# Normalisations and the last feed-forward group of a two-layer network stack, moved from between the stages into the steps around them

## The chip, the cores and the metric

The kernel runs on one core of one Trainium2 chip. The metric is the device time of one launch in microseconds. The time before is 2357.35 us, the median of 3 runs (2354.39 to 2360.7).

The core's engines run their own instruction queues in order and meet through semaphores: TensorE (PE; matrix products and transposes into the eight PSUM banks), VectorE (DVE), ScalarE (ACT), GpSimd (POOL) and SyncE (SP), which issues the DMAs here. A wait in a queue holds all that stands behind it in that queue.

## The reference

`x` is 16 batches of 128 tokens by 128 features, and so is `ctx`. All is float32.

```python
x = x + L0_xattn(layernorm(x), ctx, ctx)   # 16 heads of 8 features
x = x + L0_ffn(layernorm(x))               # "first network", depth 6
x = x + L1_xattn(layernorm(x), ctx)        # two attentions and a gate
x = x + L1_ffn(layernorm(x))               # "second network", depth 2

# one layer of a network (window 32 and 16 heads, or window 64 and 8 heads):
q, k, v = split(shift_tokens(x) @ Wqkv)    # l2-normalised q, k; rotary
x = local_attention(q, k, v) @ Wo + x
h = layernorm(shift_tokens(x)) * g + b
a, gate = split(h @ W1 + b1)               # 341 columns each
x = (a * gelu(gate)) @ W2 + b2 + x

# second cross-attention:
c2s = softmax(Qc Ks^T) Vs;  s2c = softmax(Qs Kc^T) Vc
g = sigmoid([c2s, s2c] Wg + bg);  result = g * c2s + (1 - g) * s2c
```

The layernorms in the second, third and fourth of these lines are the three "normalisations between stages" below; they have no learnt factors. Batches don't depend on each other, but a feed-forward works on a group of four batches (512 columns), and each cross-attention of the second kind on a pair (256 columns).

## The kernel before

The activations lie features by tokens in SBUF, `base_x` (the residual of a stage) and `z` (the input of a stage and the running value inside a network), each 128 partitions by 2048 columns: 16 batches, 4 groups, 8 pairs. `arena` is one large tile cut into 49 slots of 512 columns; each stage names its buffers as slots of it.

**First cross-attention.** A software pipeline over 16 batches, `for s in range(NB + 2)` on each engine (TensorE from L577 on): step s does the scores of batch s, turns probabilities of s-1 and s-2, and does the values and the output projection of s-2. `X0["res"]` counts the batches whose residual is in `base_x`.

**A normalisation between stages** (`ln_pe`, `ln_dve`, `ln_act`, L240 to L312) is done for all four groups at once: TensorE multiplies each group by a matrix of 1/128 (L231), VectorE subtracts the mean (L272), ScalarE squares (L263), TensorE gets the variances (L237), VectorE does a reciprocal square root as 11 small operations, each waiting on the last (L281 to L296, `RSQ`), TensorE spreads it over the partitions with 16 transposes (L245), and VectorE multiplies into `z` (L303). It starts when the last batch or pair of the stage before is done (`X0["res"]` is 16, `FF["outer"]` is 4, `YP["gt"]` is 32), and its banks are 0 to 7, so nothing else of TensorE goes on beside it.

**First network** (`PHASES[0]`): steps s = 0 to 103. Step s projects batch s mod 16 of layer s div 16 (L659), with rotary, norm and transposes of s-1, scores and values of s-2 and the output projection of s-3. A feed-forward group takes four steps in bank 2, from step 7 on (`ff_phase`): mean, variance and root in the first (and the down product of the group before), broadcast and first gate product in the second, two gates in the third with the gelus, three up products in the fourth. Group 23, the last, has its steps at 99 to 103, where no attention work is left. The l2 norm's Newton steps use bank 2 too (`nt`, `normal_free`). Then VectorE adds `z` to `base_x` (L1685), four times, and the normalisation follows. The transposes of the second cross-attention's weights stand there as well (L1064).

**Second cross-attention**: 11 steps over 8 pairs. Step s: projections of pair s (L1074, L1082), scores, row maximum, exponentials, row sums of s-1, values of s-1 (L1091) and outputs of s-2 (L1120), gate of s-3 (L1128; VectorE L2015 to L2023).

**Second network** (`PHASES[1]`): steps 96 to 117 with two batches a step and the feed-forward in bank 2 from step 101 on.

**SyncE** loads each batch shifted by a token from `z` into `hs` by DMA (L481, L482). Before each network it waits until all four groups of `z` are normalised (`LN["xn"]` 8 and 16).

The order of all work is written out by hand: it is the order of the calls in each engine's loops.

## Time and profile before

| | us |
|---|---|
| median of 3 runs | 2357.35 |
| profiled execution | 2356.19 |
| its span | 2354.4 |
| TensorE busy | 2149.5 |
| VectorE busy | 1740.5 |
| ScalarE busy | 1708.9 |
| GpSimd busy | 1338.4 |

The span is the time between the first and the last instruction of the profiled execution; the device time of the same execution is 1.8 us more. "Busy" is the time in which an engine had an instruction under way; it says nothing of where in the span. Views used are the page, the chain of waits (followed back from the last instruction to what released each), windows (busy time and TensorE's granted clock, as a share of 2.4 GHz, in a stretch), groups of instructions, and the timeline.

### The profile page before, as it was taken

Reading aid. Unit: us, or ns where it says so; the run is one execution under the profiler, and the core shown is the slowest. Engines: PE = TensorE matmul, PEld = TensorE weight load, DVE = VectorE, ACT = ScalarE, POOL = GpSimd, SP = SyncE. Lnnn points to the kernel's source line nnn. Section 1 sums busy time; section 2 is a strip of 40 time slices with the busy share of each in tenths; the row PEclk is TensorE's granted clock in tenths of the full one; section 3 lists DMA queues with packets and bytes.
Section 4 is the critical chain, followed back from the end, with each engine's and each line's share of the span. In section 5 each row is a group of like instructions: output and inputs, shape, how many; then the busy total and the mean of one; then the engine's idle time right before and its main releaser. Section 6 shows DMA issues by size and latency. Waiting matters only on the chain.

```text
span 2354.4 us, 88151 instructions
## 1 busy us (share of the span) xinstructions
PE 2149.5 (91%) x33770; PEld 1463.6 (62%) x33770; DVE 1740.5 (74%) x4827; ACT 1708.9 (73%) x5908; POOL 1338.4 (57%) x1270
## 2 busy tenths in 40 slices
PE   6988999999999999999999999999998696899997
PEld 4664766666666666666666666666666383566663
DVE  3868878778777777877787777778774276788873
ACT  3756878887777787778787878778876252788783
POOL 1317766666666666666676666666673033766660
PEclk8988999999999999999999999999999797999999
DMA  4001221112211221112211122112111100000000
GB/s 109 3 4 29 71 58 47 40 48 65 56 43 42 60 55 49 43 43 69 57 47 40 46 64 56 43 42 56 48 43 38 37 1 10 13 13 15 15 10 23
DMA packets 141518, 96.92 MB, mean 41 GB/s; under 512 B 61832, under 2 KB 133040, under 8 KB 141104
## 3 DMA queue, kind: packets, MB, share of 16 engines
q1 hardware_dynamic: 141104, 91.28, 15.3%
q8 instruction: 274, 4.49, 0.8%
q14 instruction: 140, 1.15, 0.2%
HBM read 23.11 MB, written 1.05 MB: 10 GB/s over the span
## 4 chain that ended last, share of the span: by engine, by line
PE 78%; issue 7%; ACT 7%; DVE 6%; POOL 2%; SPq 0%; DMA 0%; ACTq 0%; POOLq 0%; DVEq 0%
PE bank L659 22%; PE bank L770 8%; PE bank L680 7%; PE bank L737 6%; PE bank L714 5%; PE bank L828 4%; PE bank L807 4%; PE bank L723 3%; PE bank L817 3%; PE bank L708 2%; PE bank L589 2%; ACT arena L1296 1%; PE bank L597 1%; PE bank L610 1%; ACT L1296 1%
## 5 line engine op out<-in xcount | busy, mean ns | idle before, releaser
L659 PE MATMUL bank<-wqkv,hs 128*128 128x512 f32 x1344 | 673.2, 619 | 33.1 <-ACT arena L1271 15.2
L1512 POOL TENSOR_TENSOR arena<-arena,rnorm 128x512 f32<-128x512 f32 x448 | 454.3, 1042 | 382.0 <-DVE rnorm L1754 380.8
L1505 POOL TENSOR_TENSOR arena<-arena 128x512 f32<-128x512 f32 x448 | 567.0, 1273 | 168.0 <-DVE arena L1705 167.7
L1240 ACT ACTIVATE arena<-bank,amx 128x64 f32<-128x64 f32 x1536 | 457.6, 334 | 7.1 <-DVE amx L1769 6.7
L1700 DVE TENSOR_TENSOR arena<-bank,rot 128x512 f32<-128x512 f32 x448 | 307.0, 685 | 87.1 <-PE bank L659 83.1
L659 PEld LDWEIGHTS bank<-wqkv,hs 128*128 128x128 f32 x1344 | 230.2, 192 | 221.8 <-issue 160.3
L1217 ACT ACTIVATE arena<-bank 128x512 f32<-128x512 f32 x448 | 263.9, 616 | 124.1 <-PE bank L680 123.0
L1240 ACT ACTIVATION_READ_ACCUMULATOR arena<-bank,amx 128x1 f32 x1536 | 351.0, 229 | 0.0
L1705 DVE TENSOR_TENSOR arena<-bank,rot 128x256 f32<-128x256 f32 x896 | 333.8, 414 | 0.0
L1211 ACT ACTIVATE arena<-bank 128x512 f32<-128x512 f32 x448 | 264.9, 645 | 69.0 <-DVE arena L1705 68.3
L680 PEld LDWEIGHTS bank<-ident,arena 128*128 128x128 f32 x1792 | 213.3, 142 | 156.2 <-issue 125.4
L1712 DVE TENSOR_REDUCE ss<-arena 128x8 f32<-128x512 f32 x448 | 283.7, 670 | 32.5 <-ACT arena L1211 32.1
L1519 POOL TENSOR_TENSOR arena<-arena,ainv 128x512 f32<-128x512 f32 x192 | 200.2, 1043 | 160.5 <-DVE ainv L1777 160.5
L680 PE MATMUL bank<-ident,arena 128*128 128x128 f32 x1792 | 252.0, 275 | 18.3 <-POOL arena L1512 11.8
L770 PEld LDWEIGHTS bank<-arena,wo 128*128 128x128 f32 x1792 | 221.8, 195 | 55.9 <-issue 48.8
L1271 ACT ACTIVATE arena<-bank 128x256 f32<-128x256 f32 x384 | 127.2, 387 | 169.0 <-PE bank L737 168.7
L770 PE MATMUL bank<-arena,wo 128*128 128x128 f32 x1792 | 226.9, 279 | 3.3 <-ACT arena L1271 2.6
L737 PE MATMUL bank<-arena 64*64 64x32 f32 (+1 forms) x9216 | 185.4, 221 | 42.2 <-issue 41.3
L737 PEld LDWEIGHTS bank<-arena 64*64 64x64 f32 x9216 | 160.7, 135 | 67.3 <-issue 50.3
L1769 DVE TENSOR_REDUCE amx<-bank 128x4 f32<-128x256 f32 x384 | 143.9, 416 | 43.9 <-PE bank L714 43.6
L714 PE MATMUL bank<-arena 64*32 64x64 f32 (+1 forms) x12288 | 168.7, 217 | 0.0
L714 PEld LDWEIGHTS bank<-arena 64*32 64x32 f32 x12288 | 154.8, 105 | 0.2
(171 smaller groups left out, 3208.3 us busy)
## 6 DMA issues: line engine op xcount, KB each, us to landing
arena<-arena SPq DMA_DIRECT2D x768, 64.0 KB
wqkv<-in_L_ffn_Wqkv_dram SPq DMA_DIRECT2D x24, 256.0 KB, 3.2
hs<-z SPq DMA_DIRECT2D x128, 32.0 KB, 1.8
fx<-z SPq DMA_DIRECT2D x32, 128.0 KB, 2.2
hs<-z SPq DMA_DIRECT2D x128, 31.8 KB, 1.9
fx<-z SPq DMA_DIRECT2D x32, 127.0 KB, 2.5
wqkv<-in_L_ffn_Wqkv_dram SPq DMA_DIRECT2D x24, 128.0 KB, 2.6
w<-in_L_ffn_W_dram SPq DMA_DIRECT2D x6, 341.0 KB
```

What stands on the lines that cost most here:

```text
L659: nc.tensor.matmul(bank[o][:], src[:], wqkv[w][:, off:off + 512], start=True, stop=True).then_inc(AT[name] if part < 2 else AT[name][i], 1)
L680: mm = nc.tensor.transpose(bank4[o][:, j, :], rc[i][c][p % 2][:, j * P:(j + 1) * P], ident[:])
L714: mm = nc.tensor.matmul(bank[3 + g][q:q + 32, DH * j:DH * j + n], q_t[i][rows, P * j + q:P * j + q + 32], k_t[i][rows, P * j + key:P * j + ...
L737: mm = nc.tensor.matmul(bank4[7 - half][to:to + DH, j, q0:q1], src[g][rows, DH * h:DH * h + DH], pbt[i][0][rows, h * P + q0:h * P + q1], s ...
L770: mm = nc.tensor.matmul(bank4[7][:, 0, :], wo[w][:, i, j, :] if ni == 0 else wo[w][:, j // 2, j % 2, :], o_t[i][:, j * P:(j + 1) * P], sta ...
L1211: nc.scalar.activation(sq[i][c], bank[c][:], ACT.Square).then_inc(AT["sqk" if c else "sqq"], 1)
L1240: ins = nc.scalar.activation(pb[i][0][p % 2][:, h * DH:(h + 1) * DH], bank[3 + g][:, j * DH:(j + 1) * DH], ACT.Exp, bias=amx[p % 2][:, i, ...
L1505: nc.gpsimd.tensor_tensor(t, t, rs[i][c], ALU.add).then_inc(AT["ak" if c else "aq"][i], 1)
L1512: nc.gpsimd.tensor_tensor(t, t, rnorm[p % 2][:, i, HU * c:HU * c + HU].unsqueeze(2).to_broadcast([P, HU, DH]), ALU.mult).then_inc(AT["mk" ...
L1700: nc.vector.tensor_tensor(heads(rc[i][c][p % 2]), src, r[:, 2 * c, :].unsqueeze(1).to_broadcast([P, HU, DH]), ALU.mult)
L1705: ins = nc.vector.tensor_tensor(dst, src[:, :, (1 - a) * hd:(2 - a) * hd], r[:, 2 * c + 1, a * hd:(a + 1) * hd].unsqueeze(1).to_broadcast( ...
L1712: nc.vector.tensor_reduce(ss[:, i, HU * c:HU * c + HU], heads(sq[i][c]), AX.X, ALU.add).then_inc(AT["ssk" if c else "ssq"], 1)
```

## The change

Each normalisation between stages is done group by group, and its instructions are placed inside the steps of the stage before or after. The number of products, transposes and elementwise operations on full blocks is the same; the chain of 11 small VectorE operations is done once a group (4 columns wide instead of 16), so 12 times for three normalisations instead of 3. Which group goes where:

| for | groups 0 to 3 |
|---|---|
| first network | 0 in steps 6, 7, 8 of the first cross-attention; 1, 2, 3 in steps 1-2, 3-4, 5-6 of the network |
| second cross-attention | 0 and 1 in steps 96 and 97 of the first network; 2 and 3 in steps 2-3 and 5-6 of the cross-attention |
| second network | 0 and 1 in steps 7 and 9 of the cross-attention; 2 and 3 in steps 97 and 99 of the network |

Step 17 of the first cross-attention stands inside step 0 of the first network. The first network's steps end at 98; what steps 99 to 103 held (feed-forward group 23) stands in steps 1 to 5 of the second cross-attention, which gets a step without a new pair (`y_pair`) and so has 12. Its steps 10 and 11 stand behind step 96 of the second network. Buffers of the two cross-attentions get other slots of `arena`, and its values go to bank 7 instead of 2. SyncE waits for the group it needs.

```diff
-        x_q, x_k, x_v = (big[:, i * TOK:(i + 1) * TOK] for i in range(3))
+        x_q, x_k, x_v = (arena[:, (4 + i) * TOK:(5 + i) * TOK] for i in range(3))
...
+        def y_pair(t):
+            return t if 0 <= t < 6 else t - 1 if 7 <= t < 9 else -1
...
+        def g_mean(pe, n, k, o):
+            nc.tensor.matmul(bank[o][:], mean_w[:], group(base_x, k), start=True, stop=True).then_inc(LN["mean"], 1)
+        def g_var(pe, n, k, o):
+            pe.wait_ge(LN["sq"], NBLK + n + 1)
+            for j in range(4):
+                mm = nc.tensor.matmul(bank[o][:, 2 * j:2 * j + 2], g_sq[n % 2][:, j * P:(j + 1) * P], mean_w[:, 0:2],
+                                      start=True, stop=True)
+            mm.then_inc(LN["var"], 1)
+        def g_broadcast(pe, n, k, o):
+            pe.wait_ge(ln_rsqrt, (n + 2) * RSQ)
+            pe_broadcast(k, o)
...
+        def g_newton(dve, n, k, o):
+            for i in range(RSQ):
+                rsqrt(dve, i, n + 1, LN["var"], ln_rsqrt, o, 4 * k, 4 * k + 4, 0)
...
@@ SyncE, shifted_batch @@
                     if layer > ph["layer0"]:
                         sp.wait_ge(FF["z"], 4 * (layer - 1) + b // 4 + 1)
+                    else:
+                        sp.wait_ge(LN["xn"], (1 if ph["net"] == 0 else 3) * NBLK + b // 4 + 1)
...
@@ TensorE, x_step(s) of the first cross-attention @@
+                if s == 6:
+                    pe.wait_ge(X0["res"], s - 2)
+                    g_mean(pe, 0, 0, 7)
+                if s == 7:
+                    pe.wait_ge(X0["res"], s - 2)
+                    g_var(pe, 0, 0, 7)
+                if s == 8:
+                    pe.wait_ge(X0["res"], s - 2)
+                    g_broadcast(pe, 0, 0, 7)
...
@@ TensorE, first network @@
+                def group_norm(s, slot_):
+                    n = (s + 1) // 2
+                    if s % 2 == 1 and slot_ == 0:
+                        normal_free(s)
+                        pe.wait_ge(X0["res"], 4 * n + 4)
+                        g_mean(pe, n, n, 2)
+                    if s % 2 == 1 and slot_ == 2:
+                        g_var(pe, n, n, 2)
+                    if s % 2 == 0 and slot_ == 0:
+                        normal_free(s)
+                        g_broadcast(pe, n, n, 2)
...
+                    if s == 0:
+                        x_step(NB + 1)
+                        turn_weights()
...
+                    if s == hi:
+                        pe.wait_ge(AT["sqq"], un(1, hi - 1))
+                        pe.wait_ge(AT["sqk"], un(1, hi - 1))
+                        for k in range(2):
+                            pe.wait_ge(FF["outer"], k + 1)
+                            g_mean(pe, 4 + k, k, k)
+                    if s == hi + 1:
+                        for k in range(2):
+                            g_broadcast(pe, 4 + k, k, k)
...
@@ TensorE, second cross-attention: start, middle and end of step s are parts 0, 1, 2 @@
+            def between(s, part):
+                if (s, part) == (1, 1):
+                    ff0(99, 0)
+                    ff0(99, 1)
+                if (s, part) == (1, 2):
+                    ff0(99, 2)
+                if (s, part) == (2, 1):
+                    ff0(100, 0)
+                    pe.wait_ge(FF["outer"], 3)
+                    g_mean(pe, 6, 2, 6)
+                if (s, part) == (2, 2):
+                    g_var(pe, 6, 2, 6)
+                    ff0(100, 2)
+                if (s, part) == (3, 0):
+                    g_broadcast(pe, 6, 2, 6)
+                    ff0(101, 0)
+                if (s, part) == (3, 1):
+                    ff0(101, 1)
+                if s == 4:
+                    ff0(102, part)
+                if (s, part) == (5, 0):
+                    ff0(103, 1)
+                if (s, part) == (5, 1):
+                    pe.wait_ge(FF["outer"], 4)
+                    g_mean(pe, 7, 3, 2)
...
+                if s in (7, 9):
+                    n = 8 + (s - 7) // 2
+                    if part == 0:
+                        pe.wait_ge(LN["xn"], NBLK + n)
+                        pe.wait_ge(YP["gt"], 8 * (n - 7))
+                        g_mean(pe, n, n - 8, 2)
+                    if part == 1:
+                        g_var(pe, n, n - 8, 2)
+                    if part == 2:
+                        g_broadcast(pe, n, n - 8, 2)
...
+            for s in range(98):
+                t0(s)
+            y_step(0)
+            t0(98)
+            for s in range(1, 10):
+                y_step(s)
+            t1(96)
+            y_step(10)
+            y_step(11)
+            for s in range(97, 112 + 6):
+                t1(s)
```

`t0` and `t1` are a step of the first and of the second network, `ff0(s, slot)` the feed-forward's part of step s. VectorE and ScalarE have the same places with `g_centre`, `g_newton`, `g_normalise`, `g_square` and the feed-forward's operations; on ScalarE the three gelus of group 23 stand at the end of step 3. GpSimd's loops are merged in the same order, and the rotary tables of layer 0 are made in step 4 of the first cross-attention.

## Rows read from the trace of the kernel before

**Rows 1.** The page: busy time by engine; shares of the chain that ended last.

```profile
PE 2149.5 (91%) x33770; PEld 1463.6 (62%) x33770; DVE 1740.5 (74%) x4827; ACT 1708.9 (73%) x5908; POOL 1338.4 (57%) x1270
...
PE 78%; issue 7%; ACT 7%; DVE 6%; POOL 2%; SPq 0%; DMA 0%; ACTq 0%; POOLq 0%; DVEq 0%
```

**Rows 2.** Windows, first seam: from:to, length, busy by engine, TensorE clock, DMA share, GB/s.

```profile
52.00:148.00 96.00, 95.66 (x1281) 63.80 (x1280) 83.99 (x147) 73.55 (x191) 32.21 (x33) 0.95 0.01 2
...
158.30:175.60 17.30, 11.62 (x56) 9.22 (x56) 7.42 (x19) 2.52 (x4) 0.00 (x0) 0.68 0.02 4
...
175.60:199.90 24.30, 16.18 (x104) 7.15 (x104) 18.29 (x46) 6.84 (x12) 13.98 (x12) 0.71 0.03 7
...
213.70:270.30 56.60, 54.44 (x1169) 39.93 (x1169) 46.54 (x137) 48.23 (x192) 43.98 (x40) 1.00 0.25 64
```

**Rows 3.** Windows, second and third seam, with the columns of rows 2.

```profile
1793.00:1808.00 15.00, 12.41 (x330) 9.63 (x317) 6.29 (x25) 10.93 (x45) 6.09 (x6) 1.00 0.17 42
1850.00:1878.20 28.20, 18.77 (x30) 5.83 (x29) 8.17 (x12) 4.15 (x7) 0.00 (x0) 0.57 0.05 14
1878.20:1893.00 14.80, 12.39 (x57) 9.50 (x58) 6.73 (x18) 2.52 (x4) 0.00 (x0) 0.73 0.07 10
1893.00:1950.40 57.40, 49.57 (x320) 42.81 (x319) 46.12 (x81) 31.33 (x65) 22.25 (x30) 0.98 0.00 1
1950.40:1970.20 19.80, 14.17 (x56) 10.06 (x56) 7.47 (x20) 2.52 (x4) 0.00 (x0) 0.67 0.02 4
1970.20:1990.00 19.80, 13.43 (x57) 6.08 (x58) 14.07 (x36) 4.67 (x8) 9.98 (x9) 0.67 0.07 17
1996.00:2014.00 18.00, 15.11 (x148) 9.71 (x152) 13.13 (x38) 13.43 (x47) 13.84 (x14) 0.91 0.03 9
2014.00:2050.00 36.00, 31.52 (x334) 22.26 (x329) 26.68 (x75) 27.65 (x96) 26.43 (x25) 1.00 0.06 15
```

**Rows 4.** Chain of waits at the first seam: start, length, engine, what.

```profile
152.66 0.63 PE bank L597 x4
...
175.70 3.76 PE bank L659 x4
```

**Rows 5.** Timeline of two normalisations: start, length, engine, line, operation.

```profile
158.31 3.70 PE L231 MATMUL bank<-base_x,mean_w 128*128 128x512 f32 x8 [0.45 <-DVE base_x L1655]
...
161.84 4.41 PE L237 MATMUL bank<-mean_w,arena 128*128 128x2 f32 x32
...
1880.40 0.69 DVE L272 TENSOR_TENSOR arena<-base_x,bank 128x512 f32<-128x512 f32 x1 [2.30 <-PE bank L231]
...
1886.98 0.17 DVE L281 TENSOR_SCALAR lt_s<-bank 128x16 f32<-128x16 f32 x1 [2.78 <-PE bank L237]
...
1889.08 0.17 DVE L296 SCALAR_TENSOR_TENSOR rstd<-lt_b,lt_y 128x16 f32<-128x16 f32 x1
```

**Rows 6.** Timeline, last feed-forward groups of the first network, TensorE.

```profile
1840.87 1.10 PE L782 MATMUL bank<-fx,mean_w 128*128 128x512 f32 x2 [0.89 <-DVE arena L1834]
...
1842.79 2.81 PE L828 MATMUL bank<-arena,w 128*128 128x512 f32 x6 [0.83 <-issue]
...
1849.86 0.62 PE L796 MATMUL bank<-ident,fy 128*128 128x128 f32 x4 [2.35 <-DVE fy L1815]
```

**Rows 7.** Groups of instructions, VectorE, 1840.8 to 1878.2: busy, mean, idle before.

```profile
L1828 DVE COPY arena<-bank 128x512 f32<-128x512 f32 (+1 forms) x3 | 2.1, 691 | 7.4 <-PE bank L807 7.4
```

**Rows 8.** Timeline, second cross-attention (GpSimd) and start of the second network.

```profile
1924.16 1.25 POOL L1599 TENSOR_TENSOR arena<-arena,y_inv 128x512 f32<-128x512 f32 x1 [3.24 <-DVE y_inv L2007]
...
1930.02 1.25 POOL L1599 TENSOR_TENSOR arena<-arena,y_inv 128x512 f32<-128x512 f32 x1 [3.25 <-DVE y_inv L2007]
...
1970.27 3.60 PE L659 MATMUL bank<-wqkv,hs 128*128 128x512 f32 x4 [3.23 <-DMA hs<-z]
```

**Rows 9.** Timeline, ScalarE: a table load and the activations behind it.

```profile
1825.34 1.28 ACT L1296 ACT_TABLE_LOAD   x1
...
1826.63 1.95 ACT L1296 ACTIVATE arena<-arena,b 128x512 f32<-128x512 f32 x3
```

More of the change, by code:

```diff
@@ L948, in step_0 @@
                         values_all(0, s - 2)
+                    if s == hi:
+                        for k in range(2):
+                            g_var(pe, 4 + k, k, k)
                 def step_1(s):
@@ new lines, in y_step @@
+            def y_step(s):
+                new, second, third, fourth = (y_pair(s - d) for d in range(4))
+                between(s, 0)
+                if new >= 0:
+                    y_second_projections(new)
+                if second >= 0:
+                    y_scores(second)
+                if fourth >= 0:
+                    y_gate(fourth)
+                between(s, 1)
+                if third >= 0:
+                    y_probs(third)
+                if second >= 0:
+                    y_values_in(second)
+                if new >= 0:
+                    y_first_projections(new)
+                if third >= 0:
+                    y_outputs(third)
+                between(s, 2)
@@ L1454, in _, with output, between @@
-            ln_act(act, 3)
-            act_phase(PHASES[1])
+            def output(k):
+                act.wait_ge(io_ps, 2 * NBLK + k + 1)
+                nc.scalar.activation(o_st[k], bank[k % 2][:], ACT.Copy).then_inc(in_act, 1)
+            t0, ff0_square, ff0_affine, ff0_gelu = act_phase(PHASES[0])
+            t1, _a, _b, _c = act_phase(PHASES[1])
+            def between(s, part):
+                if (s, part) == (1, 1):
+                    ff0_square(23)
+                if (s, part) == (2, 1):
+                    ff0_affine(23)
+                    g_square(act, 6, 2)
+                if (s, part) == (3, 2):
+                    ff0_gelu(23)
+                if (s, part) == (5, 1):
+                    g_square(act, 7, 3)
+                if s in (7, 9) and part == 0:
+                    n = 8 + (s - 7) // 2
+                    g_square(act, n, n - 8)
@@ new lines, in y_step @@
+            def y_step(s):
+                new, second, third, fourth = (y_pair(s - d) for d in range(4))
+                between(s, 0)
+                if third >= 0:
+                    y_values_in(third)
+                if fourth >= 0:
+                    y_gate(fourth)
+                between(s, 1)
+                if third >= 0:
+                    y_probs(third)
+                if second >= 0:
+                    y_exponents(second)
+                if new >= 0:
+                    y_project(new, 1)
+                    y_project(new, 0)
+                if third >= 0:
+                    y_outputs(third, 1)
+                    y_outputs(third, 0)
+                between(s, 2)
@@ L1456, in _ @@
+            for s in range(98):
+                t0(s)
+            y_step(0)
+            t0(98)
+            for s in range(1, 10):
+                y_step(s)
+            t1(96)
+            y_step(10)
+            y_step(11)
+            for s in range(97, 112 + 6):
+                t1(s)
+                if s in (112, 113, 115):
+                    output(min(s - 112, 2))
             output(3)
@@ L1911, in step_0 @@
                         newton(s, 6, 9)
+                    if s == hi:
+                        for k in range(2):
+                            g_newton(dve, 4 + k, k, k)
                 def step_1(s):
@@ new lines, in y_step @@
+            def y_step(s):
+                new, second, third, fourth = (y_pair(s - d) for d in range(4))
+                between(s, 0)
+                if second >= 0:
+                    y_row_max(second)
+                if new >= 0:
+                    y_project(new, 0)
+                if second >= 0:
+                    y_subtract(second)
+                if fourth >= 0:
+                    y_gate(fourth, 0)
+                between(s, 1)
+                if new >= 0:
+                    y_project(new, 1)
+                if fourth >= 0:
+                    y_gate(fourth, 1)
+                if second >= 0:
+                    y_row_sum(second)
+                if fourth >= 0:
+                    y_gate(fourth, 2)
+                if second >= 0:
+                    y_inverse(second)
+                if fourth >= 0:
+                    y_gate(fourth, 3)
+                between(s, 2)
@@ L2052, in _ @@
+            for s in range(98):
+                t0(s)
+            y_step(0)
+            t0(98)
+            for s in range(1, 10):
+                y_step(s)
+            t1(96)
+            y_step(10)
+            y_step(11)
+            for s in range(97, 112 + 6):
+                t1(s)
+                if s in (111, 113, 115):
+                    outer(PHASES[1], (s - 111) // 2)
             outer(PHASES[1], 3)
```

400 lines of the change are left out of this document (226 added, 174 removed).

## The prediction

> **What bounds the kernel now.** I read the views from the whole to the seams. The page comes first [rows 1]: TensorE is busy 91% of the span, and the chain that ended last lies on it for 78%, with 7% "issue" and 6 to 7% each on VectorE and ScalarE. The windows over the first seam and the windows over the second and third [rows 2, 3] then show where this doesn't hold. In the steps of the networks and in the first cross-attention TensorE is full (95.66 of 96.00 us). At the three seams it isn't, and its granted clock is down to 0.68, 0.57 to 0.73, and 0.67 to 0.71 as means, which is 1.2 GHz for part of the time and 2.4 GHz for the rest. Seam A (first cross-attention to first network) is 153.3 to 213.7, seam B (drain of the first network to second cross-attention) 1793 to 1893, seam C (second cross-attention to second network) 1950.4 to 1996. The change works on these stretches alone; inside the 96 steps of the first network the order of instructions is the same from step 7 to step 95, so I give that part, some 1580 us, no change.
>
> **Seam A, what goes.** The last work of step 16 of the cross-attention on TensorE, four transposes, ends at 152.66 + 0.63 = 153.3 [rows 4]. From there the old kernel drains batch 15 until its first mean at 158.3 [rows 5], normalises all four groups, loads a shifted batch and starts its first projection at 175.7 [rows 4]. In the new kernel the first batches are normalised long before, so this projection can follow step 16: 175.7 - 153.3 = 22.4 us go.
>
> **Seam A, what comes.** (a) One group's normalisation inside steps 6 to 8. On VectorE it is a centring of 0.69, eleven small operations from 1886.98 to 1889.25 (2.27) and a product that I take as long as the centring, 3.65 us [rows 5]. On TensorE it is a quarter of 3.70 and of 4.41 and four transposes of 0.62 together [rows 5, 6]: 0.93 + 1.10 + 0.62 = 2.65 us. All its parts one behind another, with ScalarE's squaring as long as a centring, are 7 us. These steps wait on one another at every hand-over (VectorE 84 of 96 us), so I take 6, between 3.65 and 7. (b) Step 17 of the cross-attention now stands inside step 0 of the network, and eight weight transposes (twice the 0.62) behind it. The step's chain was 5.0 us long, 153.3 to 158.3; part of it lies beside the first rotary products. Behind the waits for it in TensorE's queue stand keys and queries of the second half of the batch, and VectorE's sums wait for those. I take 3, between 1 and 6. (c) Groups 1 to 3 in steps 1 to 6, before the feed-forward uses its bank. From 213.7 on TensorE is busy 54.4 of 56.6 us, VectorE 46.5: TensorE's 3 x 2.65 = 8 us decide; nothing would be 3 if they fill its idle time, and 14 if the waits add to them. (d) The half clock of 175.6 to 199.9 (mean 0.71) partly goes: 1, between 0 and 5. Sum: -22.4 + 6 + 3 + 8 - 1 = -6.4 us.
>
> **Seam B, steps 96 to 98.** Added are two outer sums, the normalisations of groups 0 and 1 (7.3 us of VectorE, 5.3 of TensorE, two squarings) and, after step 97, the cross-attention's first projections (eight products of 256 columns, some 2 us as 512 columns take 0.9 a pair). In the first 15 us of the drain VectorE is busy 6.3 and TensorE 12.4 [rows 3], so much of it has cover; but VectorE goes through two chains of 2.27 us at the end of step 96 while step 97 waits behind them. I take 7, between 2 and 15. The stretch then ends at 1840.8 + 7.
>
> **Seam B, the overlap itself.** From the last feed-forward group's mean at 1840.8 to the first projection of the second network at 1970.3 [rows 6, 8] are 129.5 us: 37.4 to 1878.2 for that group and the sums, 14.8 for a normalisation, 57.4 for the cross-attention, 19.8 for a normalisation and a load [rows 3]. In their place stand nine cross-attention steps with all of it inside. VectorE's work in them: 46.1 of the cross-attention, 5.8 a pair, of which the gates of the last two pairs (about half of each) and the projections of the first lie outside, so by estimate 38.6; the feed-forward group some 12 operations of the 0.69 kind [rows 7] and one root of 2.2, 10.7; four groups 14.6. That is 64 us. TensorE's: 49.6, of which by estimate 4.6 lie outside, 45; thirteen 512-column products at 0.9, from 2.81 for three of them, plus 1.7 for variance and broadcast [rows 6], 13.4; four groups 10.6. That is 69 us at full clock. A step in the steady part took 5.86 us (1924.16 to 1930.02) [rows 8], and in it VectorE does its 5.8 of a pair, without a gap, so each addition to it counts fully, and each place where the mean, the centring, the variance and the reciprocal root hand over holds it besides. I give each of nine steps 1.7 us of such waits (each of the three copies in [rows 7] was idle 2.5 us before it, at half clock for most): 64 + 15 = 79. The ends are 69, TensorE's work alone, and 100, if the two chains merely follow each other in pieces. So 79 - 129.5 = -50.5.
>
> ScalarE also changes tables twice more, because gelu now stands between exponentials. In the trace a load is 1.28 us, and the next activation starts 1.29 us after it [rows 9]: 2.6 us on an engine that is busy 31 of 57 us, so I count nothing. The Trainium skill, "ScalarE: Activation LUTs", section "What ACT_TABLE_LOAD costs", gives a switch about 2.66 us with a drain, thus 5.3 us by an estimate from that page; the trace doesn't show the second half of it, and even so it would have cover.
>
> **Seam C.** (a) The last two steps of the cross-attention now stand behind step 96, with one gate each: half of 5.86 twice is 5.9, both steps whole would be 11.7. VectorE is busy 14.1 of the first 19.8 us of the network [rows 3], so little of it is covered: 7, between 4 and 11.7. (b) Groups 10 and 11 in steps 97 and 99. Per 18 us TensorE is busy 15.1 to 15.8 there and VectorE 13.1 to 13.3 [rows 3], so part is covered: 2.5 each, 5 in all, between 0 and 9. (c) Step 96 starts at full clock: 2, between 0 and 4. Sum of B and C: 7 - 50.5 + 7 + 5 - 2 = -33.5 us.
>
> **The sum.** -6.4 - 33.5 = -39.9. The profiled execution took 2356.2 us (span 2354.4 and 1.8 around it): 2316.3. It is 1.15 below the median of the runs, 2357.35, so I forecast 2317.
>
> **Rivals.** *Waits pile up.* Engines run their queues in order, and an insertion that waits holds everything behind it. Then the nine steps take 100 and groups 1 to 3 take 14: 21 + 6 above, 2344. For it: three engines pass each small result on. Against: the parts stand in different thirds of a step. *The overlap is nearly complete*, since a wait of the one chain is work of the other: nine steps at 69, and 6 us less for seam A's insertions: 2301. Against it: VectorE had no gap in the steady part. *The clock, the case on the other side.* In the old drain the granted clock fell to 0.57 where TensorE had pauses between short products (1850 to 1878.2, [rows 3]). If it did so through steps 1 to 9, their 69 us become 138, 59 more than 79: 2376, slower than before. It decides once about two thirds of the stretch (40 of 59 us) run at 1.2 GHz. Against it: TensorE would be busy 69 of 79 us, and in the cross-attention alone (49.6 of 57.4) the clock was 0.98. The Trainium skill, "TensorE: Matmul & The Clock Gate", section "HAM oscillation — how this bites in real kernels", says that pauses within a loop can send the clock down again and again, which is this case's mechanism; by it the time would be the 2376. By that rule, the trace agrees where TensorE paused at 1850 and not where it was fed. *The change doesn't do what it says:* the new waits (the normalised groups, shared banks) let nothing start earlier and the insertions cost what the seams gave: about 2357.
>
> **How the numbers follow.** The forecast (2306 to 2330) 0.67, waits pile up (2330 to 2350) 0.12, nearly complete (2296 to 2306) 0.14, the clock 0.04, nothing 0.03. The 8 in 10 range is 2298 to 2337. About 0.3% (7 us) is what a measurement tells from no change: faster 0.93, same 0.03, slower 0.04.
>
> **What would show it.** First projection of the first network near 159; its step 3 near 207 instead of 213.7; steps 10 to 95 as long as before; the last feed-forward product of the first network inside the cross-attention; nine cross-attention steps in 79 us with VectorE over 80% busy and the clock above 0.9; first projection of the second network near 1920 and its steps from 101 on as before. I am wrong if a step of the first network is longer, if the nine steps take over 100 us, or if the clock there is below 0.8.

## The result and the profile after

The changed kernel takes 2325.15 us (median of 4 runs, 2321.75 to 2329.31) against 2357.24 (2354.39 to 2360.7): 0.9867 of the time before, 95% interval [0.9849, 0.9885], or 32.1 us less. I had forecast 2317 with 2298 to 2337. The profiled execution took 2321.82 us with a span of 2320.0, so it gained 34.4 us of span. Its page, with busy time by engine and the granted clock in 40 slices:

```profile
PE 2133.4 (92%) x33770; PEld 1456.9 (63%) x33770; DVE 1756.9 (76%) x4926; ACT 1709.5 (74%) x5910; POOL 1339.4 (58%) x1270
...
PEclk8999999999999999999999999999999998999998
```

Against [rows 1] there are 99 more VectorE instructions (nine more roots of 11) and 16.4 us more of VectorE; TensorE executes as many products in 16.1 us less busy time. Placed between the same landmarks in both traces, the 34.4 us are:

| from | to | before | after | difference | forecast |
|---|---|---|---|---|---|
| start | first feed-forward mean (seam A) | 273.3 | 263.4 | -9.9 | -6.4 |
| that | mean of group 22 (steps 7 to 95) | 1506.0 | 1518.1 | +12.1 | 0 |
| that | mean of group 23 (steps 96 to 98) | 61.5 | 58.9 | -2.6 | +7 |
| that | first projection, second network | 129.4 | 80.1 | -49.3 | -50.5 |
| that | its first feed-forward mean (seam C) | 83.9 | 95.2 | +11.3 | +10 |
| that | end | 300.3 | 304.4 | +4.1 | 0 |

The windows of the changed kernel over seam A and then over the second and third seam have the columns of [rows 2]:

```profile
52.00:154.00 102.00, 99.64 (x1296) 65.72 (x1294) 88.28 (x160) 74.30 (x194) 32.22 (x33) 0.95 0.01 3
...
158.30:213.70 55.40, 45.11 (x674) 28.39 (x674) 46.66 (x136) 32.68 (x110) 35.94 (x32) 0.94 0.08 21
213.70:263.40 49.70, 47.95 (x974) 34.40 (x958) 42.26 (x136) 39.95 (x165) 34.11 (x32) 1.00 0.26 70
```

```profile
1793.00:1808.00 15.00, 10.60 (x285) 8.44 (x285) 8.29 (x32) 9.47 (x42) 7.02 (x6) 1.00 0.15 38
1808.00:1824.00 16.00, 15.14 (x307) 11.16 (x306) 8.07 (x34) 11.00 (x48) 2.08 (x2) 1.00 0.15 36
...
1838.60:1920.40 81.80, 67.79 (x387) 53.45 (x386) 61.71 (x145) 34.61 (x67) 19.26 (x26) 0.96 0.10 25
1920.40:1978.00 57.60, 41.81 (x299) 24.93 (x297) 46.57 (x120) 29.58 (x97) 33.09 (x31) 0.88 0.03 8
```

Where [rows 3] had clocks of 0.57, 0.73 and 0.67, the nine cross-attention steps have 0.96. TensorE is busy 67.8 of 81.8 us and VectorE 61.7. The waits of TensorE in these steps (for whom, us in total, times, longest) add up to some 14 us, and no single one decides:

```profile
PE bank L250 <- DVE rstd L301: 4.6, 2, 2.4
PE bank L331 <- ACT arena L343: 3.3, 2, 2.4
PE bank L886 <- DVE arena L2043: 2.7, 1, 2.7
PE bank L886 <- issue: 1.6, 1, 1.6
```

The second network starts slower. The timeline of VectorE after its first projection (1920.46) shows why: the two last gates stand in its queue in the middle of the l2 norm's Newton steps.

```profile
1930.66 0.20 DVE L1954 TENSOR_TENSOR bank<-ny,bank 128x32 f32<-128x32 f32 x1
1930.76 0.70 DVE L2247 TENSOR_SCALAR arena<-arena 128x256 f32<-128x256 f32 x1
1931.57 1.75 DVE L2249 RECIPROCAL arena<-arena 128x256 f32<-128x256 f32 x1
...
1936.05 1.75 DVE L2249 RECIPROCAL arena<-arena 128x256 f32<-128x256 f32 x1
...
1938.75 0.19 DVE L1956 SCALAR_TENSOR_TENSOR bank<-bank,ny 128x32 f32<-128x32 f32 x1
```

The last part (from the second network's first feed-forward mean to the end), 4.1 us longer, holds the same instructions as before. In the timelines of TensorE from the last feed-forward mean on, before and then after, the same products take other times:

```profile
2326.87 1.10 PE L782 MATMUL bank<-fx,mean_w 128*128 128x512 f32 x2 [0.89 <-DVE arena L1834]
2328.80 2.81 PE L828 MATMUL bank<-arena,w 128*128 128x512 f32 x6 [0.83 <-issue]
```

```profile
2288.39 1.89 PE L840 MATMUL bank<-fx,mean_w 128*128 128x512 f32 x2 [0.89 <-DVE arena L2043]
2291.11 4.93 PE L886 MATMUL bank<-arena,w 128*128 128x512 f32 x6 [0.83 <-issue]
```

In the 7.6 us from this mean on the granted clock was 1.00 before and 0.55 after, so mostly 1.2 in place of 2.4 GHz; from the mean to the end it is 27.5 against 31.6 us.

What I had not forecast is the +12.1 us in a stretch with the same order of instructions. The experiments go to that first.

### The profile page after: what moved, and what is told of

It reads as the page before. It is cut to its first block and busy times, and to the rows that moved or that the text cites. A ratio compares the mean times of both kernels' runs of the same rounds, so it can differ in the third digit from the quotient of the medians.

```text
span 2320.0 us, 88291 instructions
## 1 busy us (share of the span) xinstructions
PE 2133.4 (92%) x33770; PEld 1456.9 (63%) x33770; DVE 1756.9 (76%) x4926; ACT 1709.5 (74%) x5910; POOL 1339.4 (58%) x1270
## 3 DMA queue, kind: packets, MB, share of 16 engines
q8 instruction: 274, 4.49, 0.9%
## 5 line engine op out<-in xcount | busy, mean ns | idle before, releaser
L715 PE MATMUL bank<-wqkv,hs 128*128 128x512 f32 x1344 | 671.2, 618 | 20.3 <-ACT arena L1438 13.8
L1919 DVE TENSOR_REDUCE ss<-arena 128x8 f32<-128x512 f32 x448 | 283.2, 669 | 32.3 <-ACT arena L1378 32.1
L795 PE MATMUL bank<-arena 64*64 64x32 f32 (+1 forms) x9216 | 186.2, 221 | 49.1 <-issue 47.4
L795 PEld LDWEIGHTS bank<-arena 64*64 64x64 f32 x9216 | 160.8, 134 | 73.5 <-issue 56.8
```

The source lines that it names most:

```text
L715: nc.tensor.matmul(bank[o][:], src[:], wqkv[w][:, off:off + 512], start=True, stop=True).then_inc(AT[name] if part < 2 else AT[name][i], 1)
L795: mm = nc.tensor.matmul(bank4[7 - half][to:to + DH, j, q0:q1], src[g][rows, DH * h:DH * h + DH], pbt[i][0][rows, h * P + q0:h * P + q1], s ...
L1919: nc.vector.tensor_reduce(ss[:, i, HU * c:HU * c + HU], heads(sq[i][c]), AX.X, ALU.add).then_inc(AT["ssk" if c else "ssq"], 1)
```

## The experiments

**Where the 12 us of the untouched steps come from.** TensorE's timeline has places where it stands 1 to 2 us in the middle of the 48 small products of the values (L795), with no semaphore to wait for ("issue"). Counted where they are over 0.5 us, between the first feed-forward mean and that of group 22, they add up to 30.8 us before (28 of them) and 37.8 after (32). Three theories: L, the stops follow from where each instruction lies in TensorE's queue, and the change moved them all; C, the change costs these steps something itself; N, they fall by chance, run by run. To tell them apart I moved the whole queue by some tiny products at its very start:

```diff
+            pe.wait_ge(c_pool, 1)
+            for _n in range(32):
+                nc.tensor.matmul(bank[7][:, 0:2], mean_w[:], mean_w[:, 0:2], start=True, stop=True)
             pe.wait_ge(ld_x, 32)
```

with 16, 32 and 48 of them in the changed kernel and 32 in the kernel before. They are not as cheap as one of the expectations below has it (some 1 us): 16, 32 and 48 take 7.0, 13.8 and 20.6 us. TensorE otherwise waits 13.5 us for its first load, so most of that costs nothing, but its own work starts 1.1 us later with 32 and 8.0 us later with 48 (changed kernel, then 32, then 48):

```profile
13.54 6.19 PE L598 MATMUL bank<-ident,arena 128*128 128x128 f32 x32 [13.54 <-DMA v_mask<-c_vmask]
```

```profile
0.99 13.81 PE L594 MATMUL bank<-mean_w 128*128 128x2 f32 x64 [0.99 <-POOL mean_w L1662]
14.67 6.10 PE L601 MATMUL bank<-ident,arena 128*128 128x128 f32 x32
```

```profile
0.99 20.64 PE L594 MATMUL bank<-mean_w 128*128 128x2 f32 x96 [0.99 <-POOL mean_w L1662]
21.50 5.40 PE L601 MATMUL bank<-ident,arena 128*128 128x128 f32 x32
```

> The changed kernel with 16 more small products (128x2, of a constant matrix) at the head of TensorE's queue, while it waits for the first loads; nothing else differs, so the work of every stage is the same. The question is why steps 7 to 95 of the first network, in which nothing was changed, took 1518.1 us (from the mean of feed-forward group 0 to that of group 22) against 1506.0 before, and the last steps of the second network 4 us more. Theory L (layout): TensorE stops for 1 to 2 us inside the block of 48 small products of the values when its instructions are not there yet, and a long stop is followed by products at half clock; where these stops fall depends on where the instructions lie in the queue, which the change shifted. Then these extra instructions move the stops, the stretch changes by 3 us or more, up or down, and the whole by as much (2310 to 2335). Theory N (chance of a run): the stretch differs from 1518.1 by less than 3 us or differs between runs of one kernel by as much as between kernels. Theory C (the change itself, by its other buffers or its waits, slows the network): stretch 1515 to 1521 whatever the shift.

> As the run with 16, with 32 more products at the head of TensorE's queue. Theory L: another stretch time than 1518.1 and than that with 16, in 1500 to 1525; the stops of over 0.5 us before the values' products come at other steps. Theory N: within 3 us of 1518.1. Theory C: 1515 to 1521.

> As the run with 16, with 48 more products at the head of TensorE's queue. Theory L: at least one of the three shifts brings the stretch down to 1510 or less and the time to about 2315 or less. Theories N and C: none does.

> The kernel before with 32 more small products (128x2) at the head of TensorE's queue. Theory L: its stretch from the mean of group 0 to that of group 22 leaves 1506.0 by 3 us or more in either direction, and its time 2356 with it (2345 to 2372). Theory N: within 3 us of both. Theory C: 1503 to 1509, since nothing of the change is in it.

Measured, in that order: 2323.51 us (0.9862, [0.9835, 0.989]); 2314.01 (0.9822, [0.9784, 0.986]); 2321.65 (0.9855, [0.9824, 0.9886]); and 2359.48 (1.0017, [1.0001, 1.0034]) for the kernel before. The stretch was 1511.9, 1508.6, 1507.5 and, before, 1512.6 us. The total with 48 has the 8.0 us of its late start in it. So C falls as an explanation of the 12 us: with another layout the changed kernel needs 1507.5, and the kernel before with another needs 1512.6. Totals overlapped, so L against N was open, and I ran the changed kernel and its copy with 32 once more on one chip.

> The changed kernel as it is, beside its copy with 32 more products on the same chip. Theory L (the 1 to 2 us stops of TensorE inside the blocks of small products follow from where instructions lie in its queue): the stops are where they were in its first profile (1.99 us at 1280.8, 2.01 at 798.8, each within a few us), the stretch from the first feed-forward mean to that of group 22 is 1518 us again, within 2, and the median stands between 2321 and 2329, 0.983 to 0.989 of the kernel before. Theory N (the stops fall where they like, run by run): they are elsewhere, and the stretch is anywhere between 1506 and 1520.

> The changed kernel with 32 tiny products (2 columns each, some 1 us at the very start) ahead of its work on TensorE, for the second time. Theory L: long stops at 453.3, 934.4 and 1659.1 again, stretch 1508.6 within 2, so about 9 us less than the changed kernel on the same chip, median 2312 to 2318. Theory N: the 2314 of the first time was the luck of four runs, and both kernels have the same median within 3 us.

The changed kernel took 2326.24 (0.9863, [0.9844, 0.9882]), its shifted copy 2315.71 (0.9812, [0.9794, 0.9831]): the intervals don't touch. The stretch was 1519.4 against 1513.3, the stops add up to 38.8 against 28.0 us. TensorE's timeline at one of the places, in the changed kernel, in its second run, and with 32 more products (first run):

```profile
1278.14 0.68 PE L795 MATMUL bank<-arena 64*64 64x64 f32 x29 [0.17 <-issue]
1280.82 0.54 PE L795 MATMUL bank<-arena 64*64 64x64 f32 x19 [1.99 <-issue]
1281.28 3.48 PE L715 MATMUL bank<-wqkv,hs 128*128 128x512 f32 x4
```

```profile
1278.63 0.68 PE L795 MATMUL bank<-arena 64*64 64x64 f32 x29 [0.17 <-issue]
1281.30 0.54 PE L795 MATMUL bank<-arena 64*64 64x64 f32 x19 [1.99 <-issue]
1281.77 3.06 PE L715 MATMUL bank<-wqkv,hs 128*128 128x512 f32 x4
```

```profile
1278.79 0.90 PE L798 MATMUL bank<-arena 64*64 64x64 f32 x48 [0.18 <-issue]
1279.62 1.98 PE L718 MATMUL bank<-wqkv,hs 128*128 128x512 f32 x4
```

The stop falls on the same product, behind the 29th of 48, in both runs, and is gone with the shift, when it stands elsewhere: at 453.3 and 934.4 us in the first run with 32 products, at 451.6 and 934.1 in the second. Behind some stops the next four 512-column products take 3.1 to 3.5 us, as here, instead of 2.0: the clock fell to 1.2 GHz for them. L holds for the places, the length of one stop is chance (1.95 and 1.40 us at 934). Six profiles have the same order on TensorE up to group 22: these two and those of the last four experiments below without a shift. The stop behind the 29th product is in all six, with 1.44 (three times), 1.72 and 1.99 us (twice). Their stops sum to 35.4 to 38.8 us and their stretches are 1512.4 to 1519.4; the three profiles of changed kernels with 32 more products have 27.0 to 30.0 and 1508.6 to 1513.3. So the layout is clear in the stops and only just in the stretch. My number for the second run's stretch, 1508.6 within 2, was missed by 4.7 us.

What is left for C can be estimated from the traces. I take from each stretch all stops of over 0.5 us ahead of products of the values and of projections, and the time that the granted clock gave away (one minus its mean, times the stretch: 10.2 us of 1518.0 after, 3.4 of 1506.0 before), as if TensorE had been at work all that time. Then 1468.0 us are left in the changed kernel and 1467.4 before, and 1467.1 to 1471.5 in all fourteen profiles, the shifted kernel before (1470.1) among them. The change itself costs these steps nothing that can be seen.

The packets of queue 8 (kind "instruction") in the window 1278 to 1284 of the changed kernel point to a cause:

```profile
q1 hardware_dynamic: 480, 0.33, 21.7%
q8 instruction: 2, 0.03, 2.3%
```

Two packets in 6 us alone say little. More is in the order of TensorE's records, the semaphore instructions counted in (70263 in the changed kernel). Numbered from 0 and divided by 256, all 464 of those stops in the fourteen profiles (432 among the values, the rest ahead of projections) leave a remainder of 193, 194 or 195: they fall at one place of every 256 records. Queue 8 moved 274 packets, one for each 256 of these records (70263 / 256 = 274.5); and behind the last packet that landed before it, each of the 432 stops ended 1.1 to 1.6 us later, where for the other products of these blocks it is anything from 0 to 10.3 us. So the engine stands, if it does, once per block of its instructions and at the same place of the count; that is shown. That it stands because the block was not there yet is the reading that fits the packets; something else that comes every 256 records, in the recording of the profile itself for instance, isn't excluded, and why one block costs 2 us and the next under 0.5 stays open. Its stops of some 0.9 us ahead of L766 are another kind: they lie elsewhere in the count and sum to 18.5 to 21.3 us in every profile. The Trainium skill, "Runtime: NRT & Kernel Launch", section "Instruction fetch mechanics", has each engine's instructions fetched in blocks of 16 KiB ahead of use and calls the cost of passing from one to the next mostly hidden, because instructions are issued slower than they arrive. On the size the profile agrees: queue 8 moved 4.49 MB in 274 packets, 16.4 KB each. On the hiding it doesn't here: 48 small products and their weight loads pass in 0.90 us, and there 2 us show.

**Seam A the old way.** Group 0's normalisation out of steps 6 to 8, groups 1 to 3 out of the network's steps, step 17 and all four groups between the stages again:

```diff
-                if s == 6:
-                    pe.wait_ge(X0["res"], s - 2)
-                    g_mean(pe, 0, 0, 7)
...
-                    if 1 <= s < 7:
-                        group_norm(s, slot_)
...
-            for s in range(NB + 1):
+            for s in range(NB + 2):
                 x_step(s)
+            ln_pe(pe, 1, base_x, lambda e, k: e.wait_ge(X0["res"], NB))
```

> The changed kernel with the first seam as it was: step 17 of the first cross-attention stands before the network, then one normalisation of all four groups, and no group's normalisation inside steps 6 to 8 or inside steps 1 to 6 of the network. The weight transposes stay in step 0. The trace of the changed kernel has the mean of feed-forward group 0 at 263.4, before it was 273.3. By the prediction's terms this seam was worth 6.4 us: group 0's mean then comes near 270; by the trace 9.9: near 273 to 274, first projection near 175.7, and the whole 10 us longer than the changed kernel (near 2332) but for stops of TensorE that fall elsewhere (6 us either way). Rival: the gain of seam A came from the weight transposes and the clock and not from the moved normalisations: group 0's mean stays below 268.

Measured 2327.78 (0.9859, [0.9822, 0.9896]). The first feed-forward mean stands at 270.4 in place of 263.4: the regrouping of seam A is worth 7.0 us. The other 2.9 of the 9.9 stay, as its first projection starts at 171.9 and not at 175.7: SyncE, which still waits for single groups here, loads the first batch earlier, and TensorE waits 0.86 us for it in place of 3.42 (before, then this run). The other 1.4 us are there already at the first mean of the normalisation, 156.9 for 158.3.

```profile
175.70 3.75 PE L659 MATMUL bank<-wqkv,hs 128*128 128x512 f32 x4 [3.42 <-DMA hs<-z]
```

```profile
171.94 3.75 PE L700 MATMUL bank<-wqkv,hs 128*128 128x512 f32 x4 [0.86 <-DMA hs<-z]
```

The rival (below 268) is out. The difference of the totals, 2.6 us, is smaller than these kernels can be told apart by.

**The last feed-forward group alone.** Steps 99 to 103 stand ahead of step 1 of the cross-attention again, on all engines; the rest as in the change.

```diff
+            for s in range(99, 104):
+                for j in range(3):
+                    ff0(s, j)
             for s in range(1, 10):
                 y_step(s)
```

> The changed kernel with the last feed-forward group of the first network (steps 99 to 103) and the sums of groups 2 and 3 run alone after step 98, before step 1 of the second cross-attention; the normalisations stay in the cross-attention's steps. From the group's mean to the first projection of the second network the changed kernel took 80.1 us. Theory of the prediction (the group costs VectorE's 10.7 us and some waits inside the steps): alone it takes 26 to 35 us and leaves the nine steps 64, so 90 to 99, and the whole is 10 to 19 us longer (2332 to 2341). Rival (in the queues' order its waits hold the cross-attention as long as it takes alone): 80 to 84, no longer than the changed kernel by more than 4 us. What the clock adds shows in the granted clock of the group's stretch, 0.57 before.

Measured 2342.19 (0.9929, [0.9907, 0.9952]). From group 23's mean to the second network's first projection it is 100.8 in place of 80.1 us: 20.7 us are this one part, of 34.4 us of span (by the medians 17.0 of 32.1). I had expected 90 to 99. Alone the group takes 33.4 us, to 1875.4, which is within the 26 to 35; the nine steps then take 67.4 us and not 64. The other 28.6 us of this stretch's gain, from the normalisations and loads that now stand inside steps, no run takes apart. Where the group is alone, the window shows TensorE busy 17.8 of 28 us at a clock of 0.65, as in [rows 3]:

```profile
1842.00:1870.00 28.00, 17.84 (x32) 5.76 (x32) 7.52 (x19) 4.89 (x6) 1.44 (x6) 0.65 0.15 39
```

**The last two steps of the cross-attention ahead of step 96.**

```diff
-            t1(96)
             y_step(10)
             y_step(11)
+            t1(96)
```

> The changed kernel with steps 10 and 11 of the second cross-attention before step 96 of the second network instead of behind it. In the changed kernel the second network goes from its first projection (1920.5) to the mean of its first feed-forward group (2015.6) in 95.2 us, before it was 83.9. Theory of the prediction (no cover in step 96; the two steps cost 7 there and 10 alone): first projection 10 us later, then 7 shorter: 3 us longer in all. Rival A (TensorE and VectorE fill each other's waits): 6 to 8 us longer. Rival B (behind step 96 they hold it up in full or more): no change, or shorter, with the stretch from projection to mean at 85 to 87.

Measured 2319.32 (0.9834, [0.981, 0.9859]). The cross-attention takes 6.0 us more, the start of the second network 3.8 less: 2.2 us worse by these landmarks. The net is near the 3 expected, but its parts are not: alone the two steps cost 6.0 us and not 10, behind step 96 they cost 3.8 and not 7. The lower median can't be given to the edit: the intervals overlap, the stretch of steps 7 to 95, which the edit doesn't touch, was 4.1 us shorter in this profile, and the end 3.3.

**No step without a new pair.** Eight pairs in eight steps, group 3's broadcast at the start of step 6.

```diff
-            return t if 0 <= t < 6 else t - 1 if 7 <= t < 9 else -1
+            return t if 0 <= t < 8 else -1
...
-                if (s, part) == (6, 1):
+                if (s, part) == (6, 0):
                     g_broadcast(pe, 7, 3, 2)
```

> The changed kernel without the step that takes no new pair: the second cross-attention takes a pair in each of steps 0 to 7 and has 11 steps; group 3 is spread and multiplied at the start of step 6 instead of its middle. Only step 10 stands behind step 96. If waits bound the steps (each has a chain of its own), one step less saves 4 to 6 us from the group's mean to the first feed-forward group of the second network; if VectorE's work bounds them, the same work stands in fewer steps and 0 to 2 us are saved. I expect 3.

Measured 2323.97 (0.9848, [0.9825, 0.987]), and from group 23's mean to the second network's first feed-forward mean 3.1 us more, where I had expected 3 less. TensorE's timeline there, and then the same broadcast in the changed kernel:

```profile
1891.75 1.12 PE L250 MATMUL bank<-ident,rstd 128*128 128x128 f32 x4 [4.00 <-DVE rstd L301]
1893.65 1.22 PE L1172 MATMUL bank<-ctx_t,yw 128*128 128x256 f32 x2 [0.78 <-DVE z L358]
...
1895.51 1.73 PE L1193 MATMUL bank<-arena 128*128 128x128 f32 x8
```

```profile
1890.05 1.14 PE L1193 MATMUL bank<-arena 128*128 128x128 f32 x8
1891.02 1.03 PE L1221 MATMUL bank<-arena,yw 128*128 128x256 f32 x4
1894.19 0.65 PE L250 MATMUL bank<-ident,rstd 128*128 128x128 f32 x4 [2.14 <-DVE rstd L301]
```

Without the empty step the next pair needs group 3 at once, and TensorE waits 4.0 us for the root with nothing to put ahead of it, after which the scores take 1.73 us at half clock in place of 1.14. The empty step is the cover of that root.

**The two gates behind the norm.** VectorE's gates of the last two pairs stand behind the Newton steps, in step 97.

```diff
@@ TensorE, step_1 @@
+                        if s == 97:
+                            pe.wait_ge(YP["ge"], 8)
                         turn(0, s - 1, 1, "mk", "kt")
@@ VectorE, step_1 @@
                         newton(s - 1, 9, 11)
...
+                    if s == 97:
+                        y_step(10)
                     if live(s):
                         rotate(0, s, 0)
+                    if s == 97:
+                        y_step(11)
```

> The changed kernel; on VectorE alone the gates of the last two pairs (steps 10 and 11 of the second cross-attention) stand in step 97 of the second network, behind the Newton steps of step 96's l2 norm instead of in the middle of them; TensorE waits for the last gate's exponentials before it writes their bank. In the changed kernel's profile the gates take VectorE from 1930.8 to 1938.75 in the middle of that chain: 8.0 us, and TensorE then waits 3.1 us for the norm. Theory G (that the gates stand in the chain is what seam C costs, term a): the norm is there 8 us earlier, some 3 of them are given back where TensorE waits for the exponentials behind the first gate, and first projection of the second network to its first feed-forward mean goes from 95.2 to about 90 (88 to 92); the end 5 us earlier, median 2319 to 2322. Rival (TensorE's own work and the half clock set this stretch): 94 to 96, no change of the end.

> The same with 32 tiny products ahead of TensorE's work. If the two gains add (10.5 us of median between the changed kernel and its shifted copy on the last chip, 5 from the gates): 2310, within 2305 to 2315, and 0.977 to 0.982 of the kernel before. If the shift was luck of the runs, no different from the kernel without it, some 2320. If only the gates fail: 2315.

Measured 2324.14 (0.9854, [0.9828, 0.988]), outside the 2319 to 2322 of theory G, and 2316.91 (0.9818, [0.9801, 0.9836]) with 32 products, where 2310 was the sum of two gains and 2315 the shift's alone. Seam C takes 93.6 us in both, for 95.2 in the changed kernel: 1.6 less, where G said 5 and its rival about nothing. The windows of this kernel, from 5.8 us ahead of the first projection on, and the second of them at the same distance from the projection in the changed kernel, show where the rest went:

```profile
1918.60:1940.00 21.40, 16.28 (x60) 12.09 (x61) 15.94 (x45) 6.99 (x14) 7.52 (x8) 0.74 0.03 7
1940.00:1960.00 20.00, 13.14 (x109) 7.88 (x107) 17.35 (x42) 8.03 (x25) 10.24 (x10) 0.72 0.03 7
```

```profile
1936.10:1956.10 20.00, 12.38 (x73) 7.10 (x72) 15.95 (x41) 7.66 (x25) 8.46 (x8) 0.81 0.03 7
```

The norm came 7.9 us earlier after the first projection (11.3 for 19.2), TensorE's transposes of the keys and queries 4.5 us earlier (18.1 for 22.6). Then VectorE is busy 17.35 of 20 us (16.0 in the changed kernel) with the gates among the next rotary products, and TensorE's clock is 0.72 for 0.81. The later place gives 1.6 us and no more; that the gates hold up something else there is the reading that fits, not a thing shown. G is right on the place and wrong on the price.

The shift's gain appears in three pairs: 2314.01, 2315.71 and 2316.91 with 32 products, 2325.15, 2326.24 and 2324.14 without. The last two pairs were measured side by side; beside the first 2314.01 stand the copies with 16 and 48 products (2323.51 and 2321.65, the latter 8.0 us late at its start). 2314.01 is the fastest median of the study; against the kernel before on the same chip the second copy is the lowest, 0.9812.

## Why the prediction held, point by point

**Seam A** (forecast -6.4, measured -9.9). The mechanism held: the first projection stands at 158.26, 0.7 us from the 159 foreseen, and term (a), 6, measured 4.9 (the last four transposes of step 16 start at 157.57 for 152.66). The first projection falls between 156.1 and 158.7 in six profiles that have this order, so a single one is good to some 2 us. Terms (b) to (d), 3 + 8 - 1 = 10, measured 7.5: from the first projection to the first feed-forward mean it is 105.1 for 97.6 us. Step 3 starts at 205.8, foreseen near 207. With the old order put back the regrouping was worth 7.0 us, close to the 6.4; the earlier load was in no term.

**Steps 7 to 95** (forecast 0, measured +12.1): the step that failed. "The order of instructions is the same" was taken to mean the same time, and one of my own marks of being wrong (a longer step of the first network) came true. The instruction order is the same; its place in the queue isn't, and the stops moved with it. The stops, those ahead of projections included, are 39.8 us for 35.1; the clock gave away 10.2 us for 3.4, in five places for two. Together that is 11.5 of the 12.1 us. How much of it is the layout and how much the one profile can't be told sharply: the clock gave away 5.1 to 11.9 us in the six profiles of one order, and the kernel before moved by 32 products, with the same stops (34.0) and five such places, took 6.6 us more. The mean stretch of the six is 1517.1, of all twelve profiles of the changed kernel and its variants 1514.6, of the two of before 1509.3. (The prediction's "some 1580 us" for this part counts from step 3; from step 7 it is 1506.)

**Steps 96 to 98** (forecast +7, measured -2.6). The single numbers mislead, because stops and falls of the clock lie here too: the old stretch took 61.5 us, and 54.3 with 32 products ahead; the new one lies between 57.8 and 62.4 in twelve profiles, with a mean of 60.2, so 2.2 above the mean of the two old ones. The sign of -2.6 comes from the clock of one old profile, which gave away 6.8 us here (before, from 1808 to 1824; after, the row of this window above has 1.00):

```profile
1808.00:1824.00 16.00, 11.59 (x183) 8.33 (x176) 2.90 (x9) 7.15 (x39) 1.04 (x1) 0.79 0.11 28
```

The shifted one gave away 1.7, the new ones 0 to 3.4. With that taken off, 54.7 and 52.6 us were old and 57.8 to 59.0 are new: an estimate of some 5 us for what was added, between the lower end (2) and the 7 taken. It takes too much off, since TensorE was not busy all the time in the old drain.

**The overlap** (forecast -50.5, measured -49.3). The nine steps took 81.8 us, and 80.1 from the group's mean, for 79. TensorE had 67.8 us of work (foreseen 69), VectorE 61.7 (64), so what VectorE waits for was 20 us and not 15; VectorE is busy 75% and not over 80%. The clock stayed at 0.96; in the second profile of the shifted kernel it is 0.90, TensorE's busy time 4.3 us longer, and the stretch from group 23's mean 84.4 for 80.1; the run with the old seam A has 0.90 and 84.4 as well. So the rival with the clock has a small true part: it costs up to some 4 us, not 59. That it mostly stayed away because TensorE was fed fits the one place where the last feed-forward group ran alone, which has 0.65.

**Seam C** (forecast +10, measured +11.3). The total is right and its terms are not, which is luck. Term (a) is visible as it was meant, 8.0 us of gates in VectorE's chain, but the two steps cost 3.8 us behind step 96 and not the 7 taken, and moving the gates gave 1.6. With the two steps ahead of step 96 the start still takes 91.3 us for 83.9, so terms (b) and (c), the normalisations of groups 10 and 11 and the clock, come to some 7.5 and not to 5 - 2 = 3. Term (c), a full clock at the start, came in part: 0.82 over the first 19.5 us, for 0.67 before. (The prediction gives the old clock of this seam as 0.67 to 0.71; [rows 3] has 0.67 for both windows, and nothing was worked out from it.)

**The end** (forecast 0, measured +4.1): 27.5 or 31.6 us from the last mean, by the clock alone. Before, it was 27.5 in both profiles; of the twelve profiles of the changed kernel and its variants, none of which alters an instruction there, five have 27.6 to 28.4, two 30.3 and 30.4, and five 31.6. So the short form exists in the changed kernel as well; whether it has become rarer can't be told from two profiles of before.

In sum -34.4 for -39.9: the seams came out 3.5 and 9.6 us better than their terms (A, and steps 96 to 98), the overlap and seam C 1.2 and 1.3 worse, and 16.2 us were lost where I had written nothing. Of these, the stretch's 12.1 are stops and falls of the clock; in single profiles a shift that computes nothing gives back 6 to 10 of them. The time came out within the likeliest case's own range (2306 to 2330), but nearer to its end than to 2317, since a term that I had set to nothing without bounds was as large as most of the terms that I had worked out. That the two better stretches, 13.1 us together, stood against it is luck: up to 6.8 of them are the clock of one old profile and not a mechanism that I had foreseen. The overlap, the largest term, is not luck.

## What to carry to other kernels

A drain stage with short products and hand-overs pays twice, in waits and in TensorE's clock, so put it inside the next stage's steps first: one feed-forward group alone was 20.7 of 34.4 us of span here. An empty step can be cheap cover for a serial chain of small VectorE operations; look what is queued at the consumer before removing it. In a kernel with tens of thousands of small products an edit anywhere moves instructions everywhere: run it with a shift or two ahead before giving a difference of half a per cent to the edit, and look in the trace how long the shift itself takes.

## What the runs showed of the hardware that I had not expected

TensorE stops for up to 2.0 us at fixed products of a dense block of small ones. The place is the same in six profiles of one order (behind the 29th of 48), the length is not (1.44 to 1.99 us). The places are 256 of TensorE's records apart, about half of those that fall among the small products cost over 0.5 us (32 of 64 in the changed kernel), and queue 8 moves one packet of 16.4 KB for each 256 records. 32 tiny products at the queue's start move them all; the sum among the values' products is 27 to 39 us of 1506 to 1520, and the median moved by 10.5 us with it. The clock often falls behind the longest: in the changed kernel its five falls to 1.2 GHz in the first network's steps follow stops of 1.71, 2.01, 1.99, 1.89 and 1.75 us (3.48 us then for four 512-column products), while another of 1.71 us, at 1768.0, has none behind it.
